# K and queries kept head by head in DRAM, and loaded with one transfer of whole rows for a half of a slot

## The reference, cut to what matters

```python
# x: [4, 2048, 256], 16 heads of 16, STRIDE = 8, MLP width 1024
def _L0_attn_ref(x, ...):
    xn = _ln(x, ln1_g, ln1_b)
    q, k, v = split(xn @ w_in.T + b_in)                 # per head
    scores = einsum('bhqd,bhkd->bhqk', q, k) / sqrt(16)
    allowed = (idx % STRIDE == 0)[:, None] | (idx[:, None] == idx[None, :])
    attn = softmax(where(allowed, scores, -inf))
    x = x + (attn @ v) @ w_out.T + b_out
    xn = _ln(x, ln2_g, ln2_b)
    return x + gelu(xn @ w1.T + b1) @ w2.T + b2

def _L0_ffn_ref(x, ...):                                # top-1 of 8 experts
    base = x @ wi_W.T + wi_b
    for i in range(8):                                  # relu(base + lora_i) @ wo_W.T, masked by the choice
        ...
x = layernorm(x + _L0_attn_ref(x)); x = layernorm(x + _L0_ffn_ref(x))
```

## Time and profile before

| what | value |
|---|---|
| median of 3 runs | 1767.41 us (1760.43 to 1771.22) |
| profiled execution: its own time | 1780.16 us |
| profiled execution: span of the trace | 1778.3 us |
| busy, share of the span: PE, PEld, DVE, ACT, POOL | 86% (1524.5 us), 63%, 48%, 41%, 37% |
| mean granted TensorE clock | 0.927 |
| DMA: mean rate, share of 16 engines' time | 74 GB/s, 22.7% |

### The profile page before, as it was taken

One profiled execution on the slowest core, in us unless ns is written; L12 is line 12 of the kernel. 1 busy time (PEld: TensorE's weight loads), 2 busy tenths in 40 slices (PEclk: granted clock), 3 DMA queues, 4 the chain that ended last, 5 costly groups with the idle time before them and its releaser, 6 DMA issues.

```text
span 1778.3 us, 26328 instructions
## 1 busy us (share of the span) xinstructions
PE 1524.5 (86%) x10166; PEld 1117.7 (63%) x10166; DVE 858.9 (48%) x1786; ACT 730.5 (41%) x1071; POOL 652.4 (37%) x536
## 2 busy tenths in 40 slices
PE   5685977889876998899987999899986999889876
PEld 4574744557765865556876865556875775555765
DVE  5643545445634545553744645543662555444221
ACT  3241444444432454345333454445342354444432
POOL 1452320034653431224862431313762442213443
PEclk8897989899998999899998998889998999899988
DMA  6542101012532101110543111110552201010100
GB/s 161 172 146 93 44 21 64 28 49 74 188 108 90 66 33 44 53 45 31 190 145 107 41 52 40 50 48 22 166 166 92 72 31 64 26 60 13 48 13 12
DMA packets 101501, 132.06 MB, mean 74 GB/s; under 512 B 17417, under 2 KB 77777, under 8 KB 98257
## 3 DMA queue, kind: packets, MB, share of 16 engines
q1 hardware_dynamic: 101376, 130.38, 22.7%
HBM read 68.87 MB, written 61.36 MB: 73 GB/s over the span
## 4 chain that ended last, share of the span: by engine, by line
PE 52%; DMA 20%; SPq 9%; DVE 9%; POOL 3%; ACT 3%; issue 2%; POOLq 0%; DVEq 0%; ACTq 0%
DMA kslot<-k_d 15%; PE ps L1366 13%; PE ps L1367 10%; PE ps L1368 10%; PE ps L1542 5%; DMA x1in<-x_d 4%; PE ps L1531 4%; SPq L784 4%; PE ps L1516 3%; SPq L779 2%; SPq L781 2%; DVE xn L1242 2%; PE ps L1578 1%; POOL rows L918 1%; PE ps L1587 1%
## 5 line engine op out<-in xcount | busy, mean ns | idle before, releaser
L1279 DVE TENSOR_REDUCE mx<-ps 128x2 f32<-128x1024 f32 x256 | 313.2, 1223 | 348.4 <-PE ps L1516 347.5
L1029 ACT ACTIVATE prob<-ps 128x1024 f32<-128x1024 f32 x256 | 262.2, 1024 | 266.8 <-PE ps L1531 266.7
L1516 PE MATMUL ps<-kslot,qslot 48*128 48x512 f32 x512 | 119.8, 463 | 107.4 <-DMA kslot<-k_d 61.3
L927 POOL TENSOR_TENSOR hid0l<-gel,hid0h 128x512 fp32r<-128x512 f32 x86 | 111.8, 1300 | 251.8 <-ACT hid0h L1071 251.8
L927 POOL TENSOR_TENSOR hid2l<-gel,hid2h 128x512 fp32r<-128x512 f32 x85 | 110.5, 1300 | 246.0 <-ACT hid2h L1071 246.0
L927 POOL TENSOR_TENSOR hid1l<-gel,hid1h 128x512 fp32r<-128x512 f32 x85 | 110.6, 1301 | 241.4 <-ACT hid1h L1071 241.4
L1063 ACT ACTIVATE gel<-ps,cols 128x512 f32<-128x512 f32 x128 | 88.2, 689 | 257.7 <-PE ps L1368 210.6
L1542 PE MATMUL ps<-prob,vals 128*32 128x256 f32 x2048 | 171.4, 408 | 2.2 <-ACT prob L1029 2.2
L1065 ACT ACTIVATE gel<-ps 128x512 f32<-128x512 f32 x128 | 76.4, 597 | 150.9 <-PE ps L1606 149.2
L1531 PE MATMUL ps<-qslot,kslot 50*128 50x256 f32 x1024 | 133.3, 340 | 3.6 <-ACT prob L1029 3.6
L1531 PEld LDWEIGHTS ps<-qslot,kslot 50*128 50x128 f32 x1024 | 79.3, 192 | 85.2 <-issue 59.1
(11 more groups left out here) (230 smaller groups left out, 4077.6 us busy)
## 6 DMA issues: line engine op xcount, KB each, us to landing
k_d<-kst SPq DMA_DIRECT2D x96, 256.0 KB, 2.6
kslot<-k_d SPq DMA_DIRECT2D x64, 384.0 KB
xin<-in_L_attn_x SPq DMA_DIRECT2D x32, 256.0 KB, 3.8
x1in<-x_d SPq DMA_DIRECT2D x16, 512.0 KB, 5.1
rows<-xs_d SPq DMA_DIRECT2D x16, 512.0 KB, 5.3
out<-rows SPq DMA_DIRECT2D x16, 512.0 KB, 4.3
y_d<-rows SPq DMA_DIRECT2D x15, 512.0 KB, 3.1
rows<-y_d SPq DMA_DIRECT2D x15, 512.0 KB, 4.1
```

Source lines behind the costliest of these rows:

```text
L927: nc.gpsimd.tensor_tensor(hid[i % RING][1][:], gel[i % 2][:], hid[i % RING][0][:], ALU.subtract).then_inc(lo_done, 1)
L1029: nc.scalar.activation(prob[(n - 1) % 2][:].rearrange("p e i q -> p (e i q)"), ps[:, 0:2, :].rearrange("p a n -> p (a n)"), ACT.Exp).then_ ...
L1279: nc.vector.tensor_reduce(best[:, :, j % NQ], ps[:, MX:MX + 2, :], AX.X, ALU.max).then_inc(maxr_done, 1)
L1516: last = mm(ps[:, MX + e, :], qslot[p % SLOTS][half, P * t:P * t + P], kslot[p % SLOTS][half, 512 * piece:512 * piece + 512], start=True, ...
```

## The change

K and queries are kept in DRAM as one array for each head, 48 rows each, in the order in which a half of a slot wants them. A load of a half is then one block of 48 whole rows. A store of K for a chunk has to lay 8 heads of 16 rows for each of the three blocks and each `m`, and becomes six transfers of 128 KB instead of three of 256 KB; the semaphore counts follow. The stores of the queries stay six, with another destination. The three first `kld` of a batch are put at items `ended + 2`, `+ 4` and `+ 6`.

```diff
@@ build_steps, projection
-                if j == ended + 2:
-                    for p in range(SLOTS):
-                        put(("kld", b, p))
+                if j in (ended + 2, ended + 4, ended + 6):
+                    put(("kld", b, (j - ended) // 2 - 1))
@@
-        k_d = nc.dram_tensor("k_d", [3, KT * P, T], F32, kind="Internal").ap()
-        q_d = nc.dram_tensor("q_d", [3, KT * P, QW], F32, kind="Internal").ap()
+        k_d = nc.dram_tensor("k_d", [H, HROWS, T], F32, kind="Internal").ap()
+        q_d = nc.dram_tensor("q_d", [H, HROWS, QW], F32, kind="Internal").ap()
@@ stk
-                    for blk, part in enumerate((0, 1, 0)):
-                        sp.dma_start(k_d[blk, :, AW * c:AW * (c + 1)].rearrange("(m p) n -> p m n", p=P),
-                                     kst[i][:, KT * part:KT * part + KT, :].bitcast(F32)).then_inc(stw[i], 16)
+                    for m in range(KT):
+                        for blk, part in enumerate((0, 1, 0)):
+                            sp.dma_start(k_d[PAIRS * m:PAIRS * (m + 1), HD * blk:HD * (blk + 1), AW * c:AW * (c + 1)],
+                                         kst[i][:, KT * part + m, :].bitcast(F32)).then_inc(stw[i], 16)
@@ stq
-                            sp.dma_start(q_d[blk, P * m:P * m + P, :], qstage[m][:, part, :].bitcast(F32)).then_inc(stq, 16)
+                            sp.dma_start(q_d[PAIRS * m:PAIRS * (m + 1), HD * blk:HD * (blk + 1), :], qstage[m][:, part, :].bitcast(F32)).then_inc(stq, 16)
@@ kld (its wait, and ACT's before it writes kst again)
-                            sp.wait_ge(stw[j], 48 * (n // 2))
+                            sp.wait_ge(stw[j], 48 * KT * (n // 2))
@@
-                                     q_d[:, HD * head:HD * head + HD, :]).then_inc(kcp[i], 16)
+                                     q_d[head]).then_inc(kcp[i], 16)
-                                     k_d[:, HD * head:HD * head + HD, :]).then_inc(kcp[i], 16)
+                                     k_d[head]).then_inc(kcp[i], 16)
```

More of the change, by code:

```diff
@@ L984, in step @@
                     if n > 2:
-                        act.wait_ge(stw[i], 48 * ((n - 1) // 2))
+                        act.wait_ge(stw[i], 48 * KT * ((n - 1) // 2))
                     if b and PLACE[a[1]] == 0:
```

## The result

The changed kernel takes **1599.09 us** (median of 3 runs, 1597.91 to 1602.01) against 1767.41 us before. The ratio of the times is 0.9056, with a 95% interval of 0.9007 to 0.9105. The forecast was 1600 us.

What follows compares the result with a forecast made beforehand. Slot loads on three engines were taken to stall PE and lower its clock. Gains 61.3 + 23.3 + 37 + 60, less 5 and 10, make 167 us: 1613 us profiled, times 0.993 gives 1600 us median, range 1568 to 1655.

Steps and rivals of the forecast that it cites:

- Loads of a slot: At a slot's first `mx`, PE's 17 waits for K vanish as loads go from 3 engines to 16: 61.3 us.
- The landing that I took: A slot's last transfer lands 5.1 us after issue, as `x1in` does; from below 2.9 us, at 310 GB/s.
- a share near 0.9 for about 3 us: Expected profile sign: DMA share during a slot's load, instead of 0.18 for 16 us.
- Ones: At a slot's first `mx`, PE's 4 waits for the slot's ones go: 23.3 us.
- Behind `x1in`: In projection tails, PE's waits caused by late `x1in` total 47.0 us; 37 counted as gained, ends 25 and 47.
- The clock: In attention and tails, PE's low clock after stalls recovers: 60 us gained, ends 35 and 78.
- Stores: In projections, new stores may run on 8 engines and land later: 5 us lost, ends 0 and 40.
- 62 us of DMA work in a 70 us stage: In a projection, eight engines need 44 us for K and query stores plus 18 for other traffic, which fits.
- Rival C: Slow stores on 8 engines make projections DMA-bound, ending slower, 1803 us at 8.5 GB/s an engine; chance 0.02.
- Returned elsewhere: Without stalls, some waits for other engines come back to PE: 10 us lost, ends 0 and 30.
- A (half given back): Stalls vanish, but clock and `x1in` return less, stores and other waits cost 50 us: 1673 us; chance 0.13.
- B (loads stay narrow): Slot loads stay near 56 GB/s, so only 0 to 20 us are gained: 1747 to 1767 us; chance 0.03.

Runs made afterwards that it cites:

- experiments 1 and 2: Kernels taking places, arrays and load width apart (1754.77 to 1598.40 us), and the changed kernel with loads walked as 3, 4 or 8 groups (1801.31, 1650.83, 1609.81 us).
- experiment 4: Changed kernel with loads to 32, 48, 64 and 128 partitions added at its end: 128 partitions (1 MB) take 4.79 us, 64 take 4.73 and 4.83 us.
- experiment 2: Changed kernel with each load's 48 rows walked as 3, 4 or 8 groups, its first dimension: 1801.31, 1650.83 and 1609.81 us.
- e4_wide_place: Kernel before, old arrays and stores, with the new places of the first loads and sources walked 16 rows first, three blocks second: 1598.40 us, ratio 0.9068.
- c4_stores: Changed kernel with each store of K cut into two of 4 heads, twelve for a chunk: 1650.28 us, ratio 0.9344.
- experiment 3: Changed kernel with each store of K cut into two of 4 heads, twelve issues for a chunk instead of six: 1650.28 us, ratio 0.9344.
- 3 groups: Changed kernel with each load's 48 rows walked as 3 groups of 16, so its first dimension is 3 again: 1801.31 us, ratio 1.016.
- e3_source_only: Kernel before with only the source of each K and query load walked 16 rows first, three blocks second: 1600.28 us, ratio 0.9038.
- e2_layout: Changed kernel with the three first loads of slots all at `ended + 2` again: 1599.08 us, ratio 0.9072.
- e1_place: Kernel before with only the three first loads put at items `ended + 2`, `+ 4` and `+ 6`: 1754.77 us, ratio 0.9945.

## Why the prediction was right, by its own steps

- **Loads of a slot, 61.3 us: right.** PE's wait for K is gone entirely, and experiments 1 and 2 tie it to the first dimension: 3 in front brings the waits back with either array. The landing that I took, 5.1 us, was good: in the changed kernel SP issues the slot's last transfer at 212.12 us and data move until about 217. The lower bound of 2.9 us was not reachable, and the sign "a share near 0.9 for about 3 us" was wrong: the share is about 1 for nearly 5 us. Both assumed that 16 engines each keep the rate of three, and 48 partitions take hardly more from 16 engines (187 GB/s) than from 8 (171). That 5.1 us came near is partly luck: it was taken from `x1in`, which writes 128 partitions and not 48, and experiment 4 shows that this matters more than the engines.
- **Ones, 23.3 us: right.** The line is gone.
- **Behind `x1in`, 37 of 47 us: a little low.** The four lines of the earlier trace rows fall by 12.2 + 13.0 + 10.1 + 9.2 = 44.5 us. DVE still waits 8.7 us in all for `x1in`, but the chain has no share left for it. `x1in` does not land in 5 to 8 us throughout, as I had written, but in 4.0 to 13.2, with a median of 6.2 us (5.1 before). The order mattered less than my text suggests: with wide loads the old places give the same time.
- **The clock, 60 us: right in size,** 57.5 us of PE's busy time. That it goes with the stalls is seen in the steps of experiment 2: with PE idle for 263, 154 and 132 us its busy time is 1541, 1485 and 1476 us.
- **Stores, 5 us: hidden, and too small to measure.** They do run on 8 engines. `e4_wide_place`, with its old stores, starts its K stores in the second batch at the same times within 0.11 us through the seventh chunk (418.06 against 418.17 us), and its first slot load 3.1 us earlier (434.35 against 437.48). That is the 3 us I named, and it is covered. My sum of 62 us of DMA work in a 70 us stage took the stage too short: from the first store to the slot's load there are 81 us, so even in `c4_stores` the chunks were not stopped. Rival C named the wrong place. Late stores reach PE first at the batch's end, through the wait of the first slot's load, not through `kst` or `xin`, and SP's time to issue them counts there before the engines do (experiment 3). My 1.4 us for SP's further issues was 3.4 - 1.4 = 2.0 us for a chunk.
- **Returned elsewhere, 10 us: too much.** The named waits fell by 61.3 + 23.3 + 44.5 = 129.1 us and idle time by 124.7, so 4.4 us came back, stores included.
- **The sum.** 61.3 + 23.3 + 44.5 + 57.5 - 4.4 = 182.2 us, where the forecast had 167: `x1in` 7.5 us more, costs 10.6 less, clock 2.5 less. For the profiled execution the forecast was 1613 us and 1597.91 were measured, 15 us less. That the median still came within 1 us is partly luck. I scaled by 0.993 because the profiled run of before was slower than its median, and the profiled run of after is not (1597.91 against 1599.09).
- **Rivals.** A (half given back) did not happen. B (loads stay narrow) is what the load with 3 groups does, and it gives 1.6% more than before, not 0 to 20 us less: the stores on 8 engines, which wide loads make up for, are then one of its costs (argued from its longer waits for ones; the last section has the rest). In rival A, ACT's share of PE's busy time in attention reads 51 to 53% from the earlier trace rows, not 51 to 54; nothing hangs on it.

No version beats the changed kernel. `e3_source_only`, `e2_layout` and `e4_wide_place` equal it within their intervals, and the first of them needs two lines.

## What to carry to other kernels

Where a load is slow at a DMA share of a few sixteenths, look at the first dimension of its access pattern before anything else: in a stretch where it moves alone, share x 16 comes near the number of engines (3.0, 4.0 and 7.4 for 3, 4 and 8 here), and reordering the walk, without touching the arrays, can be the whole cure. Then ask whether the transfer lands in time, not how fast it runs: 4 engines instead of 3 brought 150 of the 200 us that lie between 3 and 16 (1801, 1651 and 1601 us). Cutting a transfer into more pieces has a price of its own on the queue that issues them (experiment 3). And count a stall on TensorE at one and a half times its length where matmuls after it run at the lower clock (124.7 us of idle brought 57.5 us of busy time with them here, and 109.4 brought 56.2 between 3 and 4 groups).

## What the runs showed of the hardware that I had not expected

- 48 partitions take no more from 16 engines than from 8: 187 and 171 GB/s inside a slot's load, while 128 partitions take 414.
- The gap between 3 engines with the old and with the new arrays, 1754.77 and 1801.31 us (runs from 1745.33 to 1763.88 and from 1780.37 to 1807.83, on two chips). The loads in the chain took 15.5 us on average from the last issue to landing in `e1_place` (17 loads) and 16.6 us with 3 groups (18 loads); 1.1 us on 18 loads is most of the 22.5 us by which the waits for K differ (79.0 against 56.5). The waits for ones differ by 15.2 us, at the place where the stores on 8 engines land later, and PE's busy time grows as well. Why the loads themselves are slower, with rows that lie 24 KB apart instead of 8, is open; no run told the row distance from the order in which the engines meet.
- A transfer's shape sets SP's time to issue it: 0.69 us for K as 3 x 16 rows, 0.59 us as 16 x 3, 0.42 us for 48 rows (medians).
